# The last stage of a graph layer on one core: when gathers start, and how many quads behind the products the finishing steps stand

## The reference

```python
def _lap_mul(A, x):
    d = 1.0 / jnp.sqrt(jnp.sum(A, axis=-1))
    return d[:, None] * (A @ (d[:, None] * x))
z = leaky_relu(_lap_mul(A, x) @ W1 + b1, 0.1)
d2 = maximum(|z_i|^2 + |z_j|^2 - 2 z @ z.T, 0)
S = exp(-sqrt(d2 + 1e-10) / 2), kept where it is among the k = 4 largest of its row, else 0
out = _lap_mul(S + A, x) @ W2 + b2
result = layernorm(x + out)
```

## Time and profile before

| | |
|---|---|
| runs without the profiler, median (range) | 2707.34 us (2706.8 to 2710.11) |
| profiled execution, first to last instruction | 2778.3 us |
| the profiled execution over the median | 71.0 us |
| last stage in it, about | 2275 to 2778 us |
| busy in all: TensorE, VectorE, ScalarE, GpSimd | 2485.5, 2319.9, 1611.7, 1189.9 us |
| moved by DMA in all | 718 MB |

### The profile page before, as it was taken

How to read it: one execution, slowest core, us unless ns; L and a number is a source line. 1 busy time by engine, 2 the same in 40 slices (tenths; PEclk the granted TensorE clock), 3 DMA queues, 4 the chain that set the end, 5 groups by cost and what they waited for, 6 DMA issues and landing times.

```text
span 2778.3 us, 29101 instructions
## 1 busy us (share of the span) xinstructions
PE 2485.5 (89%) x9356; PEld 1727.3 (62%) x9356; DVE 2319.9 (84%) x1411; ACT 1611.7 (58%) x1911; POOL 1189.9 (43%) x981
## 2 busy tenths in 40 slices
PE   1367999999999998899999999999998987988878
PEld 0133444444677776678787777778786764666655
DVE  7998899977788888999998989989898783766766
ACT  0000000000477767899999888889898863665655
POOL 0000000000000000477778787777877966766660
PEclk9788999999999999999999999999999998998989
DMA  9999999995899850146554555555555689988875
GB/s 384 421 394 406 397 420 421 420 421 212 319 345 345 338 211 0 54 149 180 157 153 130 174 148 156 154 156 147 155 155 159 171 292 360 372 334 308 325 289 208
DMA packets 147917, 718.18 MB, mean 258 GB/s; under 512 B 19024, under 2 KB 26960, under 8 KB 86608
## 3 DMA queue, kind: packets, MB, share of 16 engines
q1 hardware_dynamic: 124384, 670.49, 64.9%
q0 software_dynamic: 18800, 37.77, 5.6%
q10 hardware_dynamic: 4608, 8.39, 0.8%
HBM read 680.40 MB, written 36.18 MB: 258 GB/s over the span
## 4 chain that ended last, share of the span: by engine, by line
PE 53%; issue 12%; DMA 10%; ACT 10%; DVE 8%; POOL 4%; another core or an unknown queue 2%; SPq 1%; POOLq 0%; ACTq 0%; DVEq 0%
PE PS L754 17%; DMA ring<-at 6%; ACT R L1123 4%; PE PS L853 4%; PE PS L855 4%; PE PS L854 4%; PE PS L953 3%; PE PS L821 3%; PE PS L817 2%; PE PS L818 2%; DMA cache<-at 2%; PE PS L894 2%; PE PS L904 2%; PE PS L895 2%
## 5 line engine op out<-in xcount | busy, mean ns | idle before, releaser
L1281 POOL TENSOR_TENSOR al<-ring,ah 128x1024 fp32r<-128x1024 f32 x264 | 637.4, 2417 | 204.1 <-ACT ah L1094 195.3
L1601 DVE MAX8 R<-R 128x8 f32<-128x8192 f32 x64 | 555.9, 8686 | 89.0 <-ACT R L1123 88.3
L1123 ACT ACTIVATE R<-PS 128x1024 f32<-128x1024 f32 x512 | 519.1, 1018 | 115.7 <-PE PS L861 83.7
L1604 DVE FIND_INDEX8 R<-R,R 128x8 uint32<-128x8192 f32 x64 | 555.9, 8685 | 0.3 <-issue 0.3
L1254 POOL CAST zst<-zh 128x128 fp32r<-128x128 f32 (+1 forms) x64 | 24.3, 380 | 1122.5 <-DVE zl L1536 814.3
L853 PE MATMUL PS<-zh,zst 128*128 128x512 f32 x1024 | 409.4, 400 | 27.0 <-ACT R L1123 15.1
L855 PE MATMUL PS<-zh,zst 128*128 128x512 f32 x1024 | 402.6, 393 | 0.0
L854 PE MATMUL PS<-zl,zst 128*128 128x512 f32 x1024 | 402.5, 393 | 0.0
L1436 POOL DMA_INDIRECT R<-xs_dram,R x256 | 280.4, 1095 | 144.8 <-issue 75.0
L1109 ACT ACTIVATE PS<-R 128x1024 f32<-128x1024 f32 x310 | 317.9, 1025 | 6.4
L1028 ACT ACTIVATE tiny<-rowsum 128x4 f32<-128x4 f32 x16 | 3.3, 205 | 485.2 <-DVE rowsum L1471 485.2
(11 more groups left out here) (169 smaller groups left out, 4322.8 us busy)
## 6 DMA issues: line engine op xcount, KB each, us to landing
R<-at SPq DMA_DIRECT2D x152, 1024.0 KB, 13.0
ring<-at SPq DMA_DIRECT2D x148, 1024.0 KB, 9.4
ring<-at SPq DMA_DIRECT2D x264, 512.0 KB, 3.9
cache<-at SPq DMA_DIRECT2D x117, 1024.0 KB, 20.6
raw_sq<-at SPq DMA_DIRECT2D x21, 1024.0 KB
raw_z<-at SPq DMA_DIRECT2D x20, 1024.0 KB
raw_ring<-at SPq DMA_DIRECT2D x20, 1024.0 KB
acc_dram<-R POOLq DMA_DIRECT2D x78, 256.0 KB, 5.7
```

The lines of the kernel that those rows point to most:

```text
L1123: act.activation(score[j % 2][:, c * EC:(c + 1) * EC].rearrange("p (b c) -> p b c", b=2), pair(first, j, c), ACT.Copy).then_inc(copied, 1)
L1281: pool.tensor_tensor(al[:, k % SPLIT], raw[k % RAW], ah[:, k % SPLIT].bitcast(F32), ALU.subtract)\
L1601: v.max(top[:, j], score[j % 2]).then_inc(dve3, 1)
L1604: v.max_index(place[:, j], top[:, j], score[j % 2]).then_inc(placed, 1)
```

## The change

Gathers are now tied to TensorE as well: the four gathers of tile j of the f-th block wait until quad `FIN_AT[f] - 16 + 7*j//4` is done (0, 1, 3 or 5 quads behind F-16). The steps of the chain get new places. ScalarE weighs at F-9, F-8, F-6 and F-4 (before F-7 to F-4), loads x at F+1 (F-3), reads a heavy sum at F+3 (F+1), takes the root at F+8 (F+6) and normalises and stores at F+10 (F+8). VectorE adds neighbours one quad behind each weighing, makes a light y at F+3 (F+1), adds the bias at F+5 (F+2), the residual at F+6 (F+4), moments at F+7 (F+5), scale and shift at F+9 (F+6). TensorE multiplies with W2 at F+4 (F+2). The seeding of a heavy block's bank follows at F+4 (F+2). The loops run on for 11 places past the last quad, which replaces the calls that stood behind them. No instruction is added or taken away but the waits on `prod_t`.

```diff
--- before.py
+++ after.py
@@ -44,6 +44,8 @@
 LAST = (G - 1) * GT // TB
 FIN = (0, 1, 9, 2, 10, 3, 11, 4, 5, 12, 6, 7, 13, 8, 14, 15)
 FIN_AT = (22, 28, 34, 41, 48, 55, 62, 69, 76, 83, 90, 97, 103, 109, 115, 123)
+GATHER_LEAD, WEIGH_LEAD = 16, 9
+XB_LAG, Y_LAG, W2_LAG, RES_LAG, ROOT_LAG, NORM_LAG = 1, 3, 4, 6, 8, 10
 OPEN_T, SUM_AFTER, ACC_AT = 6, 4, (9, 20, 40)
 SLOT = TB * BC
 PT = 2
@@ -532,6 +534,10 @@
             if place_of[u] >= 2:
                 eng.wait_ge(prod_t, halved[place_of[u] - 2] + 1)
 
+        def gathers_from(f, j):
+
+            return FIN_AT[f] - GATHER_LEAD + 7 * j // 4
+
         def wait_yf(eng, f):
 
             if FIN[f] in LIGHTS:
@@ -990,14 +996,14 @@
                                   start=True, stop=True)
                 i.then_inc(v_ok, 1)
 
-            for u in range(len(tail)):
-                quad(u)
+            for u in range(len(tail) + NORM_LAG + 1):
+                if u < len(tail):
+                    quad(u)
                 for f in range(B):
                     if u == FIN_AT[f]:
                         gathered(f)
-                    if u == FIN_AT[f] + 2:
+                    if u == FIN_AT[f] + W2_LAG:
                         times_w2(f)
-            times_w2(B - 1)
 
 
         @block.scalar
@@ -1213,11 +1219,11 @@
                     act.wait_ge(yf_heavy, n_heavy[FIN.index(ROWS_X[i] - 2)])
                 act.activation(PS[:, (ROWS_X[i] - HB) % 2], acc_x[i], ACT.Copy).then_inc(acc_seeded, 1)
 
-            for u in range(len(tail)):
-                if not plain[u]:
+            for u in range(len(tail) + NORM_LAG + 1):
+                if u < len(tail) and not plain[u]:
                     round_t(u)
                 for i, b in enumerate(ROWS_X):
-                    if u == (FIN_AT[FIN.index(b - 2)] + 2 if b - 2 in HEAVIES else FIN_AT[0] - 8):
+                    if u == (FIN_AT[FIN.index(b - 2)] + Y_LAG + 1 if b - 2 in HEAVIES else FIN_AT[0] - 8):
                         seed_heavy(i)
                 if u == BY_POOL:
                     s_of_distances(G - 1)
@@ -1225,21 +1231,18 @@
                     root_of_sums(G - 1)
                     act.wait_ge(placed, T)
                 for f in range(B):
-                    if u == FIN_AT[f] - 3:
+                    for j in range(TB):
+                        if u == FIN_AT[f] - WEIGH_LEAD + 7 * j // 4:
+                            weigh(f, j)
+                    if u == FIN_AT[f] + XB_LAG:
                         load_xb(f)
-                    if 0 <= u - FIN_AT[f] + 7 < TB:
-                        weigh(f, u - FIN_AT[f] + 7)
-                    if u == FIN_AT[f] + 1 and FIN[f] in HEAVIES:
+                    if u == FIN_AT[f] + Y_LAG and FIN[f] in HEAVIES:
                         heavy_y(f)
-                    if u == FIN_AT[f] + 6:
+                    if u == FIN_AT[f] + ROOT_LAG:
                         root_var(f)
-                    if u == FIN_AT[f] + 8:
+                    if u == FIN_AT[f] + NORM_LAG:
                         normalize(f)
                         store(f)
-            heavy_y(B - 1)
-            root_var(B - 1)
-            normalize(B - 1)
-            store(B - 1)
             for k in range(2):
                 act.wait_ge(s_out[k], 16 * B // 2)
 
@@ -1430,6 +1433,7 @@
             pool.wait_ge(s_xg_last, 16)
             for f in range(B):
                 for j in range(TB):
+                    pool.wait_ge(prod_t, gathers_from(f, j) + 1)
                     if f >= 2:
                         pool.wait_ge(gs_ok, TB * (f - 2) + j + 1)
                     for m in range(KNN):
@@ -1698,34 +1702,31 @@
 
             lk = Link(v, dve3, T)
             last_chain_a(lk)
-            for u in range(BY_POOL, len(tail)):
+            for u in range(BY_POOL, len(tail) + NORM_LAG + 1):
                 if u == BY_POOL + 1:
                     last_near_sums(lk)
                 if u == BY_POOL + 2:
                     last_scale_of_rows(lk)
                     scale_last_xg(G - 1)
-                if not plain[u]:
+                if u < len(tail) and not plain[u]:
                     rest_t(u)
                 for b in LIGHTS:
                     if u == tail.index((b, B - 1)) + SUM_AFTER:
                         light_sum(b)
                 for f in range(B):
-                    if 0 <= u - FIN_AT[f] + 6 < TB:
-                        neighbours(f, u - FIN_AT[f] + 6)
-                    if u == FIN_AT[f] + 1 and FIN[f] in LIGHTS:
+                    for j in range(TB):
+                        if u == FIN_AT[f] - WEIGH_LEAD + 1 + 7 * j // 4:
+                            neighbours(f, j)
+                    if u == FIN_AT[f] + Y_LAG and FIN[f] in LIGHTS:
                         light_y(f)
-                    if u == FIN_AT[f] + 2:
+                    if u == FIN_AT[f] + RES_LAG - 1:
                         add_bias(f)
-                    if u == FIN_AT[f] + 4:
+                    if u == FIN_AT[f] + RES_LAG:
                         residual(f)
-                    if u == FIN_AT[f] + 5:
+                    if u == FIN_AT[f] + RES_LAG + 1:
                         moments(f)
-                    if u == FIN_AT[f] + 6:
+                    if u == FIN_AT[f] + ROOT_LAG + 1:
                         scale_and_shift(f)
-            add_bias(B - 1)
-            residual(B - 1)
-            moments(B - 1)
-            scale_and_shift(B - 1)
 
 
 def kernel(x, adj, L0_gnn_W1, L0_gnn_b1, L0_gnn_W2, L0_gnn_b2):
```

## The result

| | kernel before | changed kernel |
|---|---|---|
| median (range) | 2709.74 us (2706.8 to 2714.23) | 2714.68 us (2710.62 to 2717.56) |
| ratio, 95% interval | 1 | 1.0017 [1.0011, 1.0024] |
| profiled span | 2778.3 us | 2714.0 us |

The changed kernel is slower by 0.17%, 4.9 us. The forecast was 9.0 us faster, 2698.3 us. The profiled span fell by 64 us all the same, and this is the first thing to read: a comparison of the two spans would have called the change a success.

A forecast was written before the change was run, and what follows sets the result against it. TensorE was taken to bound the last stage's long part, loads close behind, and loads its opening. -6.2 - 1.0 - 2.9 + 1.1 = -9.0 us, from 2707.3 to 2698.3 us; range 2667 to 2715 us.

The forecast's parts named there:

- Later places on VectorE: Last 14 split quads, VectorE the bound: shift brings one block's residual and moments in, pushes another's moments out, +1.1 us.
- The gathers, no wait: GpSimd's sixteen gathers a block take 20.0 us, TensorE needs 22.3 us in seven quads; no wait taken.
- Reading the sum at F+3: ScalarE's heavy read two quads later removes TensorE's 1.0 us wait in six heavy blocks, -6.2 us.
- light blocks: The later read of the sum on VectorE, which runs late anyhow: -1.0 us for all nine light blocks.
- rival C: ScalarE's `weigh` waits for late gathers, five blocks by 3.9 us: 19.5 less 9, +10.5, 2718 us; chance 0.14.
- The stalls of the profile: Last stage: most of 59 us of unmatched chain pieces likelier belongs to the profiled execution, not to timed runs.
- sign of being wrong: First step is wrong if TensorE's waits other than the long ones stay at 12 us.
- Weighing spread: ScalarE's four weighings of a block stand over six quads, not four in a row: -2.9 us.
- A: Last stage's stalls are real in timed runs too, and pacing the gathers ends them: 2673 us; chance 0.20.
- B, loads take it back: Last stage: waits removed on ScalarE become waits for loads; 2705 us, with the costs 2708; chance 0.24.
- D: Pacing the gathers changes nothing in the stalls; timed run follows the forecast, sharing its chance of 0.42.
- The end, and the load of x: Steps behind the last quad unchanged, 0; x loaded four quads later on ScalarE still has cover, 0.

The follow-up runs named there:

- both mended: Changed kernel with gathers released 20 quads ahead, not 16, and VectorE's scale and shift at F+8, not F+9: 2704.65 us, -4.3 us against the kernel before.
- second profile of before: The kernel before, unchanged, profiled once more: span 2710.2 us, time 2712.07 us.
- weighing alone: Kernel before with only the weighing at F-9, F-8, F-6, F-4 and neighbours one quad behind: 2705.66 us, -4.5 us.
- weighing with the chain mended: Kernel before with spread weighing and the chain's later places, no waits on `prod_t`, scale and shift at F+8: 2705.96 us, -3.9 us.
- halved loads: Kernel before and changed kernel, each loading only half of every piece of A from quad 12 on: 2703.09 and 2708.05 us.

## Why the prediction was wrong

**The step that failed.** The forecast was -9.0 us, the result +4.9. Two terms turned the sign. "Later places on VectorE, +1.1" priced how busy VectorE is and left out the distance from the shift to the normalising, 5.9 to 7.8 us. "The gathers, no wait" left out 1.4 to 3.3. With both mended the change gives -4.3. What is still missing against -9.0 belongs to the third failed term, "Reading the sum at F+3, -6.2" (and -1.0 for light blocks), which brought nothing that the runs show; the weighing brought 1.6 us more than forecast. That 2714.68 us lies inside the range, 0.3 us under its end of 2715, is luck: the end came from rival C at a price, 19.5 us less 9.0 of gain, of which neither part came true.

**The stalls of the profile.** Right: no timed run has them. The new span fell by 64 us while the time rose, which is what the text said would tell the two apart.

**Reading the sum at F+3, -6.2 us.** Right in the waits that it named, wrong in the price. (Six times the 1.01 us of the earlier trace rows is also 6.1, not 6.2.) ScalarE's waits for the sum fell from 17.0 us in the second profile of before to 3.7. In that profile TensorE stands behind five of these reads, like this:

```profile
2400.45 0.47 PE L963 MATMUL PS<-ah_t,xsh 128*128 128x512 f32 x1 [1.01 <-ACT ah_t L1173]
```

It is 4.3 us in the five places (1.01, 0.30, 0.99, 1.01, 1.02, the last behind the long part), and in the changed kernel they are gone. Yet TensorE's waits for roundings in the long part are 8.1 us in eight places before, 10.3 in six in the changed kernel (up to 2670 us), and 6.3 in four with both causes mended; the weighing alone, with the read early, has 5.1 in seven. So with the later places the waits are fewer and longer. Read, normalising and a weighing met in one quad of ScalarE before too, at F+1; for block 12 TensorE stands 0.99 us behind it there. Now they meet at F+3, and the mended kernel's TensorE stands 2.30 us behind the same block's read (the lines at 2562 us) and 1.39 behind another. The two other waits, 0.85 and 1.77 us, stand behind normalising and a weighing. One reason can be argued, and is not shown: at F TensorE has eight small matmuls to do while ScalarE works, at F+3 none. The times agree: weighing alone against weighing with the chain mended is -4.5 against -3.9 us, nothing gained. On ScalarE, what it no longer waits at the read (17.8 to 3.7 us between these two) it waits at the root (31.7 to 43.5). The sign of being wrong that the prediction named, TensorE's shorter waits staying at 12 us, came true: for roundings and subtractions together they are 15.7 us in the changed kernel's long part, 10.6 in that of the second profile of before. The read at F+3 was not tried without the other moves.

**Later places on VectorE, +1.1 us.** Here the sum missed the main cost. I counted what VectorE does in the last quads and looked at how far each step stands behind the products, and not at how far the steps stand from each other. The chain does not move as one piece: from shift to normalising it shrinks from two quads to one. With two quads the changed kernel differs from before by -1.0 us, with one by +4.9, with none by +31.5 (there y is read a quad earlier too). This was in the diff and needed no trace; an upper bound of the price would have been 15 blocks at one subtraction of 2.35 us.

**Weighing spread, -2.9 us.** Right in the direction, and larger: -4.5 us alone. That the forecast had half of what was left of a bound of 12 us was a guess, not a reading.

**The gathers, no wait.** Wrong in the size, right in the shape of the reserve. I took 0.95 + 0.30 = 1.25 us for a gather from single rows, 20.0 us a block. The earlier trace rows had it: 227.59 us over 204 instructions, 1.12 us each; with 0.30 that is 22.7 us a block, against 22.3 that TensorE leaves in seven quads and 18.8 in six. GpSimd is then never ahead of its release for long. What the pace takes early (all but 0.7 of the 29.1 us lie before 2532 us) is in part missing late: the last gather of the changed kernel is issued at 2672.0 us, that of the second profile of before at 2656.5. The landings take 3.9 to 7.7 us, median 5.9, so the 8.9 us of the earlier trace rows was a bound on the safe side, and the 2.15 us that the prediction estimated beside it was too short.

In the Trainium skill, Perfetto Trace Analysis, section "DMA Instruction — SWDGE (GPSIMD)", the listed end of such an instruction is when its descriptors are made, not when the data have moved. The traces agree: it is listed with 0.94 to 2.0 us, and lands after 5.9 (median).

**The rivals.** A is refuted by the second profile of before. B, loads take it back, is refuted as the bound of the stage by the halved loads, though its sign in the trace is there: waits for "DMA R<-at" on ScalarE, 21.7 us (18.8 in the second profile of before), DMA share 0.98. A full DMA share showed that loads keep pace, not that they bind. C, slower, had one of the two causes, the gathers late at `weigh` because GpSimd falls behind, in the place it named, blocks 97 to 115, but at 1.4 to 3.3 us in the changed kernel, not 19.5. The greater one was in no rival. D was right in having no effect on the time; whether the pace would end such stalls stays open, since no other execution had them, with pace or without. The chances leave B and C nothing on the faster side, though the text says "in small parts": 0.37 and 0.20 make the 0.57 already.

**The end, and the load of x, 0.** Nothing in the runs speaks against it: VectorE waits 2.0 us once for x (L1678). Neither was tried alone, so this is not shown.

## What to carry to other kernels

When a chain of steps over several engines is moved, list the distance of each consumer from its producer before and after; equal shifts of most steps hide the one pair that comes closer. Take the price of an instruction that fills an engine from its group's mean, never from the commonest instance. And look at what the moved steps meet in their new place: here waits of 1.0 us were removed, and one of 2.3 us came two quads on.

## What the runs showed of the hardware

One profiled execution held three stalls of 14.6, 13.8 and 21.1 us that none of the other 17 profiles had (the changed kernel's, the second one of before and 15 variants, spans within 6 us of the median times); no timed run shows them. The gathers, all of one shape, take 0.94 us or, in part, up to 2.0 us of GpSimd each, mean 1.10 to 1.15 over the kernels.
